# A Mamba phase on one core: three buffers for GpSimd's products, and one buffer for the fp32 matrices of both blocks in turn

## What is computed

```python
xz = einsum('bld,ed->ble', rmsnorm(x), in_w); xb, z = split(xz, 2)
xb = silu(depthwise_conv4(xb) + cb)
delta, Bm, Cm = split(einsum('ble,re->blr', xb, xp_w))
delta = softplus(einsum('blr,er->ble', delta, dtw) + dtb)
dA = exp(delta[..., None] * -exp(a_log))
mi = delta[..., None] * Bm[:, :, None, :] * xb[..., None]
def scan_fn(carry, inp):                 # one token
    v = 0.6 * v + mi_t                   # "velocity"
    h = dA_t * h + v
    y_t = einsum('ben,bn->be', h, C_t)   # product with C, summed over the 16 states
y = (ys + dp * xb) * silu(z);  x = x + einsum('ble,de->bld', y, ow)
```

## Time and profile before

| | |
|---|---|
| median of the runs | 4501.99 us (4496.07 to 4504.96) |
| the profiled execution | 4487.59 us, its span 4485.9 us |
| busy: PE, DVE, ACT, POOL | 3543.9, 2774.5, 1980.0, 2046.1 us |
| granted TensorE clock, mean | 0.866 |
| the two Mamba phases | about 1000 to 3672 us of the span |
| in them: products (L898), 512 | 1205.4 us busy, 2355 ns each |

### The profile page before, as it was taken

How to read it: one execution, slowest core, us unless ns; L and a number is a source line. 1 busy time by engine, 2 the same in 40 slices (tenths; PEclk the granted TensorE clock), 3 DMA queues, 4 the chain that set the end, 5 groups by cost and what they waited for, 6 DMA issues and landing times. The chain is left out here.

```text
span 4485.9 us, 88366 instructions
## 1 busy us (share of the span) xinstructions
PE 3543.9 (79%) x28412; PEld 2364.3 (53%) x28413; DVE 2774.5 (62%) x4814; ACT 1980.0 (44%) x4446; POOL 2046.1 (46%) x1206
## 2 busy tenths in 40 slices
PE   6888869936898888888856988889888863199980
PEld 4554546614555555555534555555555543188870
DVE  3444432345777777777765777777777767255545
ACT  1212112215666565665625666566565633133320
POOL 0101000014666676666744667676676764500006
PEclk8888878967999999999987999999999985599995
DMA  4000000012223121231211212122121223311113
GB/s 143 0 0 0 0 21 0 0 56 55 59 53 76 49 74 52 52 74 48 74 38 45 69 50 73 51 60 66 51 73 51 62 74 106 141 47 47 49 37 109
DMA packets 152098, 244.93 MB, mean 55 GB/s; under 512 B 25714, under 2 KB 74130, under 8 KB 149012
## 3 DMA queue, kind: packets, MB, share of 16 engines
q1 hardware_dynamic: 142356, 212.69, 17.4%
q0 software_dynamic: 9344, 27.27, 1.8%
HBM read 119.89 MB, written 38.27 MB: 35 GB/s over the span
## 5 line engine op out<-in xcount | busy, mean ns | idle before, releaser
L898 POOL TENSOR_TENSOR m_hc<-m_h,m_Cb 128x1024 f32<-128x1024 f32 x512 | 1205.4, 2355 | 763.5 <-DVE m_h L1019 466.2
L1019 DVE TENSOR_TENSOR_SCAN m_h<-m_dA,m_hlast,m_bank 128x256 f32<-128x256 f32 x2048 | 1354.2, 725 | 140.1 <-PE m_bank L1300 74.0
L1282 PE MATMUL m_bank<-m_hc,ident 128*128 128x512 f32 x2048 | 1207.7, 679 | 148.5 <-POOL m_hc L898 148.3
L1149 ACT ACTIVATE m_dA<-m_delta,m_rate 128x256 f32<-128x256 f32 x2048 | 894.1, 500 | 16.4 <-DVE m_h L1019 15.4
L1298 PEld LDWEIGHTS m_bank<-m_M,m_U 128*128 128x128 bf16 x8192 | 605.0, 101 | 358.3 <-DVE m_h L1019 222.2
L1298 PE MATMUL m_bank<-m_M,m_U 128*128 128x64 bf16 x8192 | 674.9, 197 | 124.5 <-DVE m_h L1019 117.0
L1300 PEld LDWEIGHTS m_bank<-m_M,m_U 112*128 112x128 bf16 x8192 | 578.5, 100 | 204.5 <-issue 172.6
L1300 PE MATMUL m_bank<-m_M,m_U 112*128 112x64 bf16 x8192 | 675.2, 197 | 0.0
L1282 PEld LDWEIGHTS m_bank<-m_hc,ident 128*128 128x128 f32 x2048 | 337.3, 204 | 198.0 <-POOL m_hc L898 164.9
L967 DVE SCALAR_TENSOR_TENSOR m_cv<-m_xpre,m_conv,m_cv 128x256 f32<-128x256 f32 x384 | 273.3, 753 | 22.6 <-ACT m_cv L1087 18.1
L1212 PE MATMUL m_bank<-m_pair,m_in 128*128 128x256 f32 x1024 | 268.7, 389 | 8.2 <-ACT m_cv L1087 4.4
(11 more groups left out here) (260 smaller groups left out, 5594.2 us busy)
## 6 DMA issues: line engine op xcount, KB each, us to landing
m_Cb<-m_c_rows SPq DMA_DIRECT2D x256, 256.0 KB, 3.2
m_M<-m_Mhi SPq DMA_DIRECT2D x128, 256.0 KB, 4.1
m_M<-m_Mlo SPq DMA_DIRECT2D x64, 256.0 KB, 3.9
m_U<-m_Uhi SPq DMA_DIRECT2D x128, 128.0 KB, 3.3
slots_x<-x_res SPq DMA_DIRECT2D x40, 256.0 KB, 3.0
x_x_in<-slots_x SPq DMA_DIRECT2D x40, 256.0 KB, 2.6
slots_y<-x_y POOLq DMA_DIRECT2D x40, 256.0 KB, 2.3
m_U<-m_Ulo SPq DMA_DIRECT2D x64, 128.0 KB, 3.6
```

The source lines that it names most:

```text
L898: nc.gpsimd.tensor_tensor(hc[:, n % 2], h[:, n % RING], Cb[:, g % 2, n % NG, :].unsqueeze(1).broadcast_to([P, KI, CM]), ALU.mult).then_inc ...
L1019: nc.vector.tensor_tensor_scan(h[:, n % RING, m, :], dA[:, n % RING, m, :], VB[(n % 2) * 2 + g][:, (m % 2) * CM:(m % 2 + 1) * CM], hlast[: ...
L1149: nc.scalar.activation(dA[:, n % RING, m, :], delta[:, par, m, :], ACT.Exp, scale=rate[:, m, n:n + 1]).then_inc(s["da_done"], 1)
L1282: last = nc.tensor.matmul(Y[half][:], net.ident[:], hc[:, n % 2, 2 * half:2 * half + 2, :], start=(n == 0), stop=(n == NS - 1))
```

## The change

`hc` gets a third buffer and `Mf` loses the half for block 1: both are 4 KB a partition. Products, and PE's accumulations, take buffer (n + par) % 3. A product then waits for the accumulation three states back; in even chunks states 0 and 1 still wait for that two states back, since the 16 states of a chunk aren't a multiple of three. Since both blocks use one `Mf`, the second `Mf` must wait for the first `Mlo`, which has to wait for the first `Mhi`: POOL's `Mlo` of block 0 goes from at = 25 to 24 and `Mf` of block 1 from 23 to 25, both then in slot 7; ACT's `Mhi` of block 0 goes from 24 to 23, into slot 6. The passing of `par` through `accumulate` and `late` is left out below.

```diff
-        Mf = sb("Mf", [P, TM, NS, SUB])
+        Mf = sb("Mf", [P, NS, SUB])
-        hc = sb("hc", [P, 2, KI, CM])
+        hc = sb("hc", [P, 3, KI, CM])
                 def matrix(q, j):
                     pool.wait_ge(s["b_done"], 1 + q + 1)
-                    nc.gpsimd.tensor_tensor(Mf[:, j], decay_n, Bs[:, j, :].unsqueeze(2).broadcast_to([P, NS, SUB]),
+                    pool.wait_ge(s["mlo_done"], 1 + q * TM + j)
+                    nc.gpsimd.tensor_tensor(Mf[:], decay_n, Bs[:, j, :].unsqueeze(2).broadcast_to([P, NS, SUB]),
                                             ALU.mult).then_inc(s["mf_done"], 1)
...
                         matrix(q, 0)
-                    if at == 23:
+                    if at == 24:
+                        matrix_low(q, 0)
+                    if at == 25:
+                        pool.wait_ge(s["mlo_done"], 1 + q * TM + 1)
                         matrix(q, 1)
-                    if at == 25:
-                        matrix_low(q, 0)
...
                     pool.wait_ge(s["scan_done"], 1 + AHEAD + (k + 1) * KI + next_scan)
-                    pool.wait_ge(s["acc_done"], 1 + AHEAD + k - 1)
+                    pool.wait_ge(s["acc_done"], 1 + AHEAD + k - (1 if par == 0 and n < 2 else 2))
...
-                    nc.gpsimd.tensor_tensor(hc[:, n % 2], h[:, n % RING],
+                    nc.gpsimd.tensor_tensor(hc[:, (n + par) % 3], h[:, n % RING],
...
-                    if at in (24, 27):
-                        j = (at - 24) // 3
+                    if at in (23, 27):
+                        j = (at - 23) // 4
                         act.wait_ge(s["mf_done"], 1 + q * TM + j + 1)
                         act.wait_ge(s["m_moved"], 1 + 6 * 16 * q)
-                        nc.scalar.copy(Mhi[:, j], Mf[:, j]).then_inc(s["mhi_done"], 1)
+                        nc.scalar.copy(Mhi[:, j], Mf[:]).then_inc(s["mhi_done"], 1)
```

More of the change, by code:

```diff
@@ L730, in _ @@
                     at = SUB + part * NS
-                    sp.dma_start(Mf[at:at + NS, 0], dram["decay"][SUB:SUB + NS]).then_inc(s["loaded"], 16)
+                    sp.dma_start(Mf[at:at + NS], dram["decay"][SUB:SUB + NS]).then_inc(s["loaded"], 16)
                     sp.dma_start(Gf[at:at + NS, 0], dram["carry_on"]).then_inc(s["loaded"], 16)
@@ L848, in matrix_low @@
                     pool.wait_ge(s["m_moved"], 1 + 6 * 16 * q)
-                    nc.gpsimd.tensor_tensor(Mlo[:, j], Mf[:, j], Mhi[:, j], ALU.subtract).then_inc(s["mlo_done"], 1)
+                    nc.gpsimd.tensor_tensor(Mlo[:, j], Mf[:], Mhi[:, j], ALU.subtract).then_inc(s["mlo_done"], 1)
                 def head(q, par, at):
@@ L937, in _ @@
                     for j in range(NSUB):
-                        nc.vector.tensor_copy(M2[SUB:SUB + 2 * NS, par, j], Mf[SUB:SUB + 2 * NS, 0])
-                        nc.vector.tensor_copy(M2[SUB + 2 * NS:KV, par, j], Mf[SUB + 2 * NS:KV, 0])
+                        nc.vector.tensor_copy(M2[SUB:SUB + 2 * NS, par, j], Mf[SUB:SUB + 2 * NS])
+                        nc.vector.tensor_copy(M2[SUB + 2 * NS:KV, par, j], Mf[SUB + 2 * NS:KV])
                 on = Gf[:, 0].rearrange("p i n -> p (i n)")
@@ L945, in _ @@
                     for j in range(NSUB):
-                        nc.vector.tensor_tensor(M2[SUB + 2 * NS:KV, par, j], Mf[SUB + 2 * NS:KV, 0],
+                        nc.vector.tensor_tensor(M2[SUB + 2 * NS:KV, par, j], Mf[SUB + 2 * NS:KV],
                                                 M2[SUB + 2 * NS:KV, par, j], ALU.subtract)
@@ L1274, in tail, with accumulate @@
                             last.then_inc(s["out_psum"], 1)
-                def accumulate(c, n, half):
+                def accumulate(c, par, n, half):
                     k = c * NS + n
@@ L1281, in accumulate @@
                         pe.wait_ge(s["gate_done"], 1 + c * KI + 2 * half + 2)
-                    last = nc.tensor.matmul(Y[half][:], net.ident[:], hc[:, n % 2, 2 * half:2 * half + 2, :],
+                    last = nc.tensor.matmul(Y[half][:], net.ident[:], hc[:, (n + par) % 3, 2 * half:2 * half + 2, :],
                                             start=(n == 0), stop=(n == NS - 1))
@@ L1302, in velocity, with late @@
                     last.then_inc(s["v_psum"], 1)
-                def late(c, n, half):
+                def late(c, par, n, half):
                     if not (isinstance(c, int) and c == 0):
-                        accumulate(c - 1, n + NS - 2, half)
+                        accumulate(c - 1, 1 - par, n + NS - 2, half)
                 def slots(c, par, more, more2):
@@ L1316, in slots @@
                             if at < 2:
-                                late(c, 0, g)
+                                late(c, par, 0, g)
                             elif at == 2:
-                                late(c, 1, 0)
-                                late(c, 1, 1)
+                                late(c, par, 1, 0)
+                                late(c, par, 1, 1)
                             elif n > 2:
-                                accumulate(c, n - 2, g)
+                                accumulate(c, par, n - 2, g)
                             elif at == 5:
-                                accumulate(c, 0, 0)
-                                accumulate(c, 0, 1)
+                                accumulate(c, par, 0, 0)
+                                accumulate(c, par, 0, 1)
                             tail(c, 1 - par, at, more)
@@ L1345, in _ @@
                 for n in range(2):
-                    late(NCM, n, 0)
-                    late(NCM, n, 1)
+                    late(NCM, 0, n, 0)
+                    late(NCM, 0, n, 1)
                 tail(NCM, 1, 7, False)
```

## The result

The changed kernel takes 4516.87 us (median of 13 runs, 4510.14 to 4523.49), the kernel before, run beside it, 4490.92 (13 runs, 4480.94 to 4504.96). The ratio is 1.0065, 95% interval 1.0053 to 1.0076: slower by 26 us, or 24 to 34 by the interval. The prediction said 4536 against a median before of 4501.99, which is 1.0076: the sign and the mechanism held, and the size was at the upper edge.

A forecast was written before the change was run, and what follows sets the result against it. PE was taken to bound the kernel, so only its idle places count. Mid-chunk 33.3 us plus layer starts 1.0 made 34.3, other parts 0: from 4501.99 to 4536 us, range 4484 to 4562 (own range 4520 to 4562).

The forecast's parts named there:

- POOL's row: Mid-chunk, slots 6 to 9: product 6 starts 0.7 us earlier, Mlo 2.32 later, L979 waits for Mlo, product 7 follows Mf.
- the race: Mid-chunk, whether product 7 (starting 1817.10) or L984 (ready 1817.30) goes first; product 7 forecast to win by 0.20 us.
- The term: POOL's new order mid-chunk: L984 takes 3.23 us against a mean of 2.12, losing 1.11 in 30 chunks, 33.3 us.
- The starts of the layers: At each of two layer starts, L984 waits and ends at 1035.5 in place of 1035.02: 0.5 us each, 1.0 together.
- PE's first wait: PE's idle time at 1818.35 for product 7, forecast to grow from 2.18 to 3.3 us.
- PE's other two waits: PE's idle times for state 9's scans (1.13 us) and product 8 (1.38), forecast unchanged because both sides move.
- my own sign of being wrong: The forecast would be wrong if L979 still went ahead of Mlo, or PE showed idle time in the full stretches.
- The clock: PE runs at 1.2 GHz for a while behind idle times; effect bounded at -15 to +27 us, taken as 0.
- the case that I bounded at -0.5 us a chunk: Half of the added 1.1 us of PE idle time falls into slow-clock time; the bound's low end, -15 us.
- my first rival: Mid-chunk, L984 goes ahead of product 7, gaining 0.3 to 0.7 us a chunk, 9 to 21: 4487; chance 0.17.
- The third buffer's rival: Where chunks meet, DVE sets the pace; the freed convolution gives up to 60 us, less 34 lost: 4476; chance 0.04.
- What signs I named: Profile: L984 about 3.2 us, shorter Mlo and convolutions, longer second Mf, POOL's PE wait nearly gone, PE's product waits up a third.

## Why the prediction was right, step by step

- PE, not POOL, sets the end, and the waits that a third buffer removes hold up nobody: right. The third buffer alone removes 64 of 70 waits and gives 1.0005.
- POOL's row, counted from the start of the six scans: product 6 at +1.08 (measured 1.02), `Mlo` +3.40 (3.34), L979's end +6.62 (6.56), `Mf`'s end +8.38 (8.33), product 7 +8.34 (8.29), L984 ready +8.54 (8.56). The margin of the race was put at 0.20 us and is 0.27. Each figure came off by 0.06 or less, and nearly all to one side.
- L984 at 3.23 us: 3.15 in this chunk, and (97.7 - 2 x 1.81) / 30 = 3.14 in the mean. The loss at its end is 1.03 us a chunk (before rounding; 11.60 against 10.58), where I put 1.11. The term is 31 us in place of 33.3.
- The starts of the layers: 8.30 us from the clamp's end to L986's, 7.90 before, so 0.4 us in place of 0.5 for each.
- The single `Mf`'s wait at no cost: right, and shown by the two kernels that have it or not (1.0065 and 1.0056, whose intervals overlap).
- PE's first wait grows to 3.3 us: 3.28. "PE's other two waits stay as they are, nothing gives the 1.11 back" failed in part. The 1.13 us wait for the scans of state 9 is gone, that for product 8 is 1.11 in place of 1.38, and a new one, 1.27 for `u`, stands at 1844.49, in a stretch where I had PE full: that PE shows idle time in the full stretches was my own sign of being wrong, and for this part of the sum it came true. Total waits shown in this chunk are 5.66 us, and 2.18 + 1.13 + 1.38 before with 0.32 for `u`: 5.01.
- The clock. Busy time by stretch, from product 7's arrival to about slot 10, of the kernel before and then of the changed one:

```profile
1818.35:1826.60 8.25, 5.42 (x39) 2.36 (x40) 8.22 (x13) 5.55 (x15) 6.21 (x4) 0.82 0.58 130
```
```profile
1836.35:1843.50 7.15, 5.76 (x38) 2.83 (x38) 7.12 (x11) 4.60 (x13) 5.12 (x3) 0.76 0.64 131
1843.50:1868.00 24.50, 23.50 (x231) 15.71 (x232) 17.20 (x27) 14.31 (x41) 20.35 (x12) 0.93 0.46 117
```

  Before, a pair is that slow only at 1824.11, behind the waits for state 9 and product 8 (2.08 us; the earlier trace rows show its first matmul). After the longer idle time (3.28 us) the granted clock falls earlier: two matmuls take 2.06 us at 1838.14, the level of 1.2 GHz, where before the pair in that place took 1.10:

```profile
1819.82 1.10 PE L1282 MATMUL m_bank<-m_hc,ident 128*128 128x512 f32 x2
```

  Those slow matmuls run where PE used to wait for the scans, and the stretch behind is at 0.93 in place of 0.92. That is the case that I bounded at -0.5 us a chunk and did not take: it fits the sign of PE's 6.3 us less of busy time. No run separates the clock from the order of the waits, so how the missing 6 us (34.3 against 28) divide between it and the 2 us of the smaller term stays open.
- The race lost by product 7, my first rival, did not come about in this kernel, but its mechanism is real: it is what the order alone does in 22 of 30 chunks, and there its time was 0.9990, where I had put 4487 against 4502, 0.9967. That total is a mixture: the 8 lost chunks are longer than the same ones before and hide a part of what the 22 give. With the single `Mf` and two buffers the 22 last 79.09 us from clamp to clamp, and the same 22 last 79.92 in the kernel before; of the lost ones, six lie whole in a layer, and last 80.25 against 78.61. So a gain of 0.3 to 0.7 us a chunk wasn't too high, although PE's wait for product 7 grows from 2.2 to as much as 4.7 us there; a single chunk varies by more than 1 us, so the 0.8 is rough. What I had wrong is where the race decides: not at `Mf`'s end behind 1817.30, but some 0.1 us later (the last section has the figures).
- The third buffer's rival (4476) fell with its own run.

What signs I named held, but for three. PE's idle time in a full stretch is told above. POOL's wait for PE isn't nearly gone: there are 7 in place of 70, but of up to 9.8 us, 57.7 in all. And PE's wait for products rose by 18%, not by a third.

## What to carry to other kernels

Before removing an engine's waits, ask which instruction the end hangs on; here it is one DVE instruction a chunk, and the kernels' times stand in the order in which that one ends. Where two engines take turns at SBUF, read who is running when the late instruction becomes ready and what is queued behind: a quarter of a microsecond decided whether 26 us were lost or none. When a change frees an engine and the kernel gets slower, look for the pair that the freed engine now runs ahead of, and look at the awaited instruction's last input, not only at the engine in the way. An earlier input pays only where it wins the turn: on the changed kernel it was worth about 1.1% (1.0065 to 0.9952), on the kernel before nothing.

## What was not expected of the hardware

Near a tie the turn isn't settled by a program's order. In the kernel with two buffers and the new order, L986 ends 9.73 us behind the clamp in 22 chunks and 11.9 in the other 8 of the same profile, with nothing different in the program between them. The starts differ by hundredths of a microsecond. L986 starts first in all 30, while `Mf` still runs: in the 22 product 7 starts 0.05 to 0.07 us behind it and `Mf` ends 0.09 to 0.11 behind it, in the 8 it is 0.02 to 0.05 and 0.06 to 0.09, and product 7 goes ahead all the same. The new order alone shows the same split. With `Glo` ahead of product 7 the 24 won chunks have product 7 0.12 to 0.14 us behind L986, the 6 lost 0.05 to 0.06. So the rule that a waiting DVE instruction takes the next turn has an edge. Where product 7 started less than 0.05 us behind L986 it went ahead every time, and where it started more than 0.06 behind, L986 did. Why is not shown.

And the scans, which read one input from SBUF, are not held up by a product that runs beside them: six take 3.93 us beside product 6 in the changed kernel as they did beside `Mf` and the product before.
